# A macaron block on one core: where the bulk loads stand, three additions for four, and attention's head in the written-out order

## The reference

```
x = x + 0.5 * ffn(layernorm(x))
x = x + attn(layernorm(x))
x = x + 0.5 * ffn(layernorm(x))

ffn:  top 2 of 8 experts per row (softmax over the two logits), each expert 512 -> 256 -> gelu -> 512,
      plus a shared expert 512 -> 512 -> gelu -> 512
attn: z = causal conv, width 4, of x @ W_mem: k (32 heads x 8) and one score per head
      p = exp(clip(score) + decay);  phi = k * theta, 8 frequencies per value
      cs = cumsum(p, p*cos(phi), p*sin(phi)) over the 512 rows of a batch's sequence
      out_re = sum over m of (re*q_re + im*q_im) / den,  out_im = sum over m of (im*q_re - re*q_im) / den
      y = out_re @ W_re + out_im @ W_im per head;  y = value * silu(gate);  return y @ W_out
```

## Time and profile before

| | |
|---|---|
| median of 3 runs | 1228.48 us |
| lowest to highest | 1225.8 to 1231.84 us |
| the profiled execution, its own time | 1230.61 us |
| its span | 1229.1 us |
| TensorE busy | 1027.5 us, 84% |
| VectorE busy | 727.2 us, 59% |
| ScalarE busy | 658.5 us, 54% |
| GpSimd busy | 485.3 us, 39% |
| TensorE's granted clock, mean | 0.939 of full speed |

### The profile page before, as it was taken

The page is one execution under the profiler, slowest core; times in us unless marked ns, Lnnn a source line. Parts: engine busy times, 40 slices in busy tenths (PEclk is TensorE's granted clock), DMA queues, the critical chain, the costliest instruction groups (busy, mean ns, idle before and its releaser), DMA issues. The chain is left out here.

```text
span 1229.1 us, 11345 instructions
## 1 busy us (share of the span) xinstructions
PE 1027.5 (84%) x3424; PEld 563.1 (46%) x3424; DVE 727.2 (59%) x1206; ACT 658.5 (54%) x1112; POOL 485.3 (39%) x452
## 2 busy tenths in 40 slices
PE   4939999858999679799878979987978898679993
PEld 2526545534445445344534534444555543336661
DVE  3500016699799699689969977897979920300000
ACT  2414325578556487454866774446579851314441
POOL 4335431353533443250733312634364420165552
PEclk9969999988999889989979989899989999789997
DMA  8886571666744666843765827256686663125666
GB/s 274 320 283 113 98 163 50 170 150 119 159 126 117 181 154 109 210 115 101 202 155 106 208 77 171 53 169 139 137 188 148 101 121 70 58 64 109 112 111 103
DMA packets 68976, 172.53 MB, mean 140 GB/s; under 512 B 12354, under 2 KB 12354, under 8 KB 66790
## 3 DMA queue, kind: packets, MB, share of 16 engines
q0 software_dynamic: 32576, 72.44, 32.6%
q1 hardware_dynamic: 36342, 99.38, 26.7%
HBM read 112.86 MB, written 68.33 MB: 147 GB/s over the span
## 5 line engine op out<-in xcount | busy, mean ns | idle before, releaser
L859 PE MATMUL yps<-w_all,hidden_sb 128*128 x424 | 210.7, 621 | 43.6 <-ACT hidden_sb L1025 43.5
L843 PE MATMUL hps<-w_all,hidden_sb 128*128 x848 | 209.3, 391 | 22.5 <-ACT hidden_sb L1025 18.4
L1612 POOL DMA_INDIRECT xs<-x_normal,rows_i x106 | 131.7, 1242 | 210.4 <-PE xps L834 159.5
L843 PEld LDWEIGHTS hps<-w_all,hidden_sb 128*128 128x128 f32 x848 | 161.2, 195 | 76.5 <-issue 58.7
L1414 DVE TENSOR_TENSOR_SCAN run<-pwx,trig 128x512 f32<-128x512 f32 x128 | 149.2, 1206 | 12.8 <-ACT trig L1111 12.5
L1636 POOL DMA_INDIRECT x_rows<-ys,rows_i x56 | 100.1, 1788 | 119.3 <-ACT ys L1038 110.3
L859 PEld LDWEIGHTS yps<-w_all,hidden_sb 128*128 128x128 f32 x424 | 79.5, 197 | 120.5 <-issue 117.9
L1038 ACT ACTIVATE ys<-yps,slots 128x512 f32<-128x512 f32 x106 | 72.8, 689 | 96.2 <-PE yps L859 86.6
L801 PE MATMUL yps<-sw_sb,hidden_sb 128*128 128x512 f32 x256 | 123.9, 628 | 0.0
L789 PE MATMUL hps<-xnT,sw_sb 128*128 128x512 f32 x256 | 118.2, 610 | 0.7 <-ACT hidden_sb L998 0.7
L834 PE MATMUL xps<-ident,xs 128*128 128x128 f32 x424 | 66.5, 281 | 41.1 <-DMA xs<-x_normal,rows_i 33.5
(11 more groups left out here) (200 smaller groups left out, 1597.3 us busy)
## 6 DMA issues: line engine op xcount, KB each, us to landing
qx<-q_cols SPq DMA_DIRECT2D x128, 256.0 KB
x_normal<-xin SPq DMA_DIRECT2D x32, 256.0 KB, 4.1
w_all<-in_w_experts SPq DMA_DIRECT2D x8, 1024.0 KB, 7.3
xin<-x_rows SPq DMA_DIRECT2D x32, 256.0 KB, 7.1
turns_sb<-in_w_out SPq DMA_DIRECT2D x3, 1536.0 KB, 12.7
xin<-in_x SPq DMA_DIRECT2D x16, 256.0 KB, 4.6
sum_rows<-ys SPq DMA_DIRECT2D x16, 256.0 KB, 4.1
xin<-sum_rows POOLq DMA_DIRECT2D x16, 256.0 KB, 9.0
```

Source lines behind the costliest of these rows:

```text
L843: t = PE.matmul(hps[:, bank, 0:H], xT[:, j % 2, c, :], w_all[:, bass.ds(expert[j] + c * H, H)], start=c == 0, stop=c == KC - 1)
L859: t = PE.matmul(yps[:, bank, :], hb[:, j % 2, ec, :], w_all[:, bass.ds(expert[j] + (KC * H + ec * D), D)], start=ec == 0, stop=ec == EC - 1)
L1612: GE.indirect_dma_start(xs[:, j % NX, :], None, xn_rows[PAIR_OF[g]], bass.IndirectOffsetOnAxis(rows_i[:, g % 2, j:j + 1], 0)).then_inc(*xs ...
```

## The change

Three things. First, the start: `tables` is split. What the gate and the placement need is made first (last signal `consts` 5), the rest in `more_tables` (`consts` 6 for the zero rows, 15 the last). The expert loads go out from the first weights on, one ahead of the normalised rows' store; the block-diagonal weights and the copies of batches 1 to 3 wait for the third block's first product. Group 0's copy stands behind the experts. The scatters are planned in fours, group 1's behind `bring(0, 2)`. Second, the sums: `add_parts` does the imaginary part first and writes the real part into the other half of `qx`, so that `sum_parts` adds both with one 1,024-wide addition; the wait of a step's phases is on the additions, two steps before, for the sum. Third, all pieces of attention's head get 2,000 more in `way`.

```diff
@@ plan_weights, plan_job, plan_blocks
-            piece("POOL", ("w_rest",), 9.0, ("POOL", ("load", 0)))
+            piece("POOL", ("w_tables",), 3.0, ("POOL", ("load", 0)))
+            piece("POOL", ("w_rest",), 6.0, ("POOL", ("w_tables",)))
-                piece("SP", ("w_expert", e), 0.6, *([("SP", ("w_expert", e - 1), 4.0)] if e else [("SP", ("w_rest",))]))
-            piece("SP", ("w_bd",), 0.5, ("SP", ("w_expert", E - 1)))
+                piece("SP", ("w_expert", e), 0.6, ("SP", ("w_expert", e - 1) if e else ("w_first",), 4.4))
+            piece("SP", ("w_bd",), 0.5, ("PE", ("one", 0, 2)))
-                piece("SP", ("w_rows", b), 0.5, ("SP", ("w_expert", E - 1) if b else ("w_bias",)))
+                piece("SP", ("w_rows", b), 0.5, ("PE", ("one", 0, 2)) if b >= len(GROUPS[0]) else ("SP", ("w_expert", E - 1)))
-            piece("POOL", ("scatter", g), 2.5 * GTS[g], ("DVE", ("place", g)), *[("DVE", ("gates", q)) for q in GROUPS[g]],
-                  ("SP", ("w_rest",), 3.0))
+            for i in range(GTS[g] // 2):
+                piece("POOL", ("scatter", g, i), 5.1, ("DVE", ("place", g)), *([("POOL", ("bring", 0, 2))] if g == 1 else []),
+                      *[("DVE", ("gates", q)) for q in GROUPS[g]], ("SP", ("w_rest",), 3.0))
@@ plan_step
-            piece("DVE", ("c_sum", b, n), 2.8 if m else 1.4, ("DVE", ("c_times", b, n)),
+            piece("DVE", ("c_sum", b, n), 2.6 if m else 1.4, ("DVE", ("c_times", b, n)),
@@ orders
+            for k in work:
+                if k[1][0] in ("a_load", "a_stats", "a_norm", "a_turn", "a_mem", "a_p", "a_fall", "a_q", "a_spread"):
+                    way[k] += 2000.0
@@ tensor_program
                 pe.wait_ge(*small_loaded.at(2))
-                pe.wait_ge(*consts.at(16))
                 pe.wait_ge(*x_kept.at((q, TB - 1)))
@@ vector_program
-                    vec.wait_ge(*(out_summed if last[1] % M else added).at((*last, 0)))
+                    vec.wait_ge(*added.at((*last, 0)))
             def add_parts(b, n):
-                re = outT[:, half, 0, :] if m == 0 else re2[:, 0, :]
-                im = outT[:, half, 1, :] if m == 0 else im2[:, 0, :]
+                re, im = [outT[:, half, i, :] if m == 0 else im2[:, i, :] for i in range(2)]
                 if m == 0 and b > 0:
                     vec.wait_ge(*y_made.at((b - 1, half * VH + VH - 1)))
-                vec.wait_ge(*real_made.at((b, n)))
-                VE.tensor_tensor(re, re2[:, 0, :], re2[:, 1, :], ALU.add).then_inc(*added.of((b, n, 0)))
                 vec.wait_ge(*imag_made.at((b, n)))
                 VE.tensor_tensor(im, im2[:, 0, :], im2[:, 1, :], ALU.subtract).then_inc(*added.of((b, n, 1)))
+                vec.wait_ge(*real_made.at((b, n)))
+                vec.wait_ge(*added.at((b, n, 1)))
+                VE.tensor_tensor(re, re2[:, 0, :], re2[:, 1, :], ALU.add).then_inc(*added.of((b, n, 0)))
             def sum_parts(b, n):
-                re, im = outT[:, half, 0, :], outT[:, half, 1, :]
                 vec.wait_ge(*added.at((b, n, 0)))
-                VE.tensor_tensor(re, re, trig[:, n % 2, 0, :], ALU.add).then_inc(*out_summed.of((b, n, 0)))
-                vec.wait_ge(*added.at((b, n, 1)))
-                VE.tensor_tensor(im, im, qx[:, n % NQX, 0, :], ALU.add).then_inc(*out_summed.of((b, n, 1)))
+                VE.tensor_tensor(outT[:, half, :, :], outT[:, half, :, :], qx[:, n % NQX, :, :],
+                                 ALU.add).then_inc(*out_summed.of((b, n)))
@@ sync_program
                 elif stage == "w_bd":
+                    sp.wait_ge(*one_made.at((0, 2)))
                     SP.dma_start(wbd_sb[:, :, :, :], w_bd).then_inc(*bd_loaded.of(0))
                 elif stage == "w_rows":
+                    if at[0] >= len(GROUPS[0]):
+                        sp.wait_ge(*one_made.at((0, 2)))
```

More of the change, by code:

```diff
@@ L316, in plan_job @@
             rows, turned_rows = rows_free(("fetch", q))
-            start = [("SP", ("w_first",), 7.0), ("SP", ("w_bias",), 2.5), ("POOL", ("w_rest",))] if q == 0 else []
+            start = [("SP", ("w_first",), 7.0), ("SP", ("w_bias",), 2.5), ("POOL", ("w_tables",))] if q == 0 else []
             x_rows = [("POOL", ("o_rows", b, tb), 3.6) for tb in range(TB)] if f == 2 else []
@@ L362, in plan_blocks @@
             piece("PE", ("place", g), 2.2, ("DVE", ("rank", z)), bank=[("xps", ("DVE", ("place", g)))])
-            piece("DVE", ("place", g), 6.5, ("PE", ("place", g)),
-                  *([("PE", ("two", g - 2, NBS[g - 2] - 1)), ("POOL", ("scatter", g - 2), 2.0)] if g > 1 else []))
-            piece("POOL", ("scatter", g), 2.5 * GTS[g], ("DVE", ("place", g)), *[("DVE", ("gates", q)) for q in GROUPS[g]],
-                  ("SP", ("w_rest",), 3.0))
-            piece("SP", ("slots", g), 0.5, ("POOL", ("scatter", g), 3.0),
+            piece("DVE", ("place", g), 5.0 if NB < 16 else 6.5, ("PE", ("place", g)), *([("DVE", ("rows", 0))] if g == 1 else []),
+                  *([("PE", ("two", g - 2, NBS[g - 2] - 1)), ("POOL", ("scatter", g - 2, GTS[g - 2] // 2 - 1), 2.0)] if g > 1 else []))
+            for i in range(GTS[g] // 2):
+                piece("POOL", ("scatter", g, i), 5.1, ("DVE", ("place", g)), *([("POOL", ("bring", 0, 2))] if g == 1 else []),
+                      *[("DVE", ("gates", q)) for q in GROUPS[g]], ("SP", ("w_rest",), 3.0))
+            piece("SP", ("slots", g), 0.5, ("POOL", ("scatter", g, GTS[g] // 2 - 1), 3.0),
                   *([("ACT", ("two", g - 2, NBS[g - 2] - 1)), ("DVE", ("rows", g - 2))] if g > 1 else []))
@@ L769, in gate_logits @@
                 bank = bank_of(xps_turn, ("logits", q))
+                pe.wait_ge(*consts.at(5))
                 pe.wait_ge(*chunks_kept.at(q))
@@ L1451, in scale_output @@
                 vec.wait_ge(*spread_den.at((b, half)))
-                vec.wait_ge(*out_summed.at((b, half * M + M - 1, 1)))
+                vec.wait_ge(*out_summed.at((b, half * M + M - 1)))
                 if half:
@@ L1670, in tables @@
                 GE.tensor_tensor(chunk_sum[:, :], chunk_pairs[:, 0, :], chunk_pairs[:, 1, :], ALU.add)
+                GE.memset(earlier[:, :], 1.0).then_inc(*consts.of(2))
+                GE.memset(before[:, :, :], 1.0).then_inc(*consts.of(3))
                 GE.memset(half_pi[:, :], math.pi / 2)
@@ L1677, in tables @@
                 GE.memset(gcols[:, :, 2 * (E + 1):BR], 0.0)
-                GE.memset(no_rows[:, :, 1], 0.0)
-                GE.memset(earlier[:, :], 1.0).then_inc(*consts.of(2))
-                GE.memset(before[:, :, :], 1.0).then_inc(*consts.of(3))
-                GE.memset(rep_sb[:, :], 1.0).then_inc(*consts.of(4))
                 GE.iota(steps_of[:, :], pattern=[[P, E]], base=0, channel_multiplier=0,
@@ L1692, in tables @@
                             allow_small_or_imprecise_dtypes=True)
+                pool.wait_ge(*consts.at(3))
+                GE.affine_select(out=earlier[:, :], in_=earlier[:, :], compare_op=ALU.is_gt, fill=0.0, base=0,
+                                 pattern=[[1, P]], channel_multiplier=-1).then_inc(*consts.of(4))
+                GE.affine_select(out=before[:, :, :], in_=before[:, :, :], compare_op=ALU.is_gt, fill=0.0, base=0,
+                                 pattern=[[1, E], [-1, E]], channel_multiplier=0).then_inc(*consts.of(5))
@@ L1695, in tables @@
                 GE.iota(posn, pattern=[[1, T]], base=0, channel_multiplier=0,
-                        allow_small_or_imprecise_dtypes=True).then_inc(*consts.of(6))
-                pool.wait_ge(*consts.at(6))
-                GE.affine_select(out=earlier[:, :], in_=earlier[:, :], compare_op=ALU.is_gt, fill=0.0, base=0,
-                                 pattern=[[1, P]], channel_multiplier=-1).then_inc(*consts.of(7))
-                GE.affine_select(out=before[:, :, :], in_=before[:, :, :], compare_op=ALU.is_gt, fill=0.0, base=0,
-                                 pattern=[[1, E], [-1, E]], channel_multiplier=0).then_inc(*consts.of(8))
+                        allow_small_or_imprecise_dtypes=True).then_inc(*consts.of(9))
@@ L1735, in pool_program @@
                     own = a_norming.at((at[0], 7))
+                elif stage == "w_tables":
+                    pool.wait_ge(*own)
+                    tables()
+                    own = consts.at(5)
                 elif stage == "w_rest":
                     pool.wait_ge(*own)
-                    tables()
-                    own = consts.at(16)
+                    more_tables()
+                    own = consts.at(15)
                 elif stage == "scatter":
```

73 lines of the change are left out of this document (36 added, 37 removed).

## The result

| | before | changed |
|---|---|---|
| median | 1229.57 us | 1259.72 us |
| lowest to highest | 1225.8 to 1231.84 us | 1257.75 to 1265.54 us |
| ratio | | 1.0256, 95% interval 1.0213 to 1.0299 |
| span of the profiled execution | 1229.1 us | 1257.9 us |

The change makes the kernel 2.6% slower. I had forecast 1222 us with 1241 as the upper end, so the result lies far outside.

The account below looks back on a forecast made before the run. TensorE was taken to bound the first batch's blocks, VectorE to be nearest a bound in the running sums (107 us idle). -10 + 11 - 5 - 3 = -7 on 1230.6 us, less 2.1 for the median: 1222 us, range 1203 to 1241.

Parts of the forecast that it names:

- The start (-10): Start of the kernel: first block 22.3 us sooner, less 12 us for moved loads; net -10 us, bounds -22 and -3.
- The 10.4 us for the bulk loads: Batch 0's blocks: gathers beside the moved 6.3 MB land after 14.4 us against 4.0; the 10.4 us taken once.
- my 12 us: Batch 0's blocks: cost of the start's move, 10.4 us for bulk loads and 1.6 for scatters between adds.
- The sums (+11): VectorE's running sums: dependent additions at 0.11 us a wait make 17 us, a third falls into idle; bounds +5 and +17.
- The rival in which the waits are free: VectorE's running sums: waits on its own signals cost nothing, VectorE -3 for +11, giving 1208 us; chance 0.1.
- Heads first (-5): Attention's head earlier on all engines: -17 for row waits, +12 for the last head; together -5 us, bounds -20 and +12.
- I take half of the two, -17: VectorE in the running sums: half of its 18.9 us wait for input rows and 15.5 for summed rows is saved.
- The exposed last head, +12: Batch 3's head, after step 47 and its scaling: VectorE idles 15 us for 3.68, +12 us.
- The tail (-3): From last scaling to last group's first block: 118 us and some 2 of gaps for 122.7; -3 us, bounds -5 and +8.
- The slow rival: VectorE's queue gets longer everywhere: +16 us gives 1244.5, or 1238 if a third of the removed waits is real; chance 0.23.
- the idle time above 107 us: Running sums: VectorE's idle time staying above 107 us would decide for the slow rival.
- the 120 that I had named as a sign of being wrong: Running sums: the forecast is wrong if VectorE's idle time there is under 80 or over 120 us.

Follow-up runs that it names:

- e5: Kernel before with only the new start, old additions, no heads first, later order written out as before: 1218.35 us beside 1229.18, ratio 0.9914.
- e8: Kernel before with only the new start, old additions, no heads first, in the order the planner finds: 1213.5 us, ratio 0.9882.
- e12: The start alone in planner's order, with the bulk loads waiting for the twelfth block's first product instead of the third's: ratio 0.9866.
- e11: Kernel before, its four 512-wide additions resequenced so each sum stands right behind the part it adds; all other order same: ratio 1.0026.
- e2: Kernel before with the three additions for the four and nothing else, in its own order: 1240.5 us, ratio 1.0055.
- e6: Kernel before with the new start and the three additions, no heads first, later order written out as before: 1225.34 us, ratio 0.9957.
- e7: Kernel before with 2,000 more in `way` for all pieces of attention's head and nothing else: ratio 1.0286.
- e10: Kernel before, order written out: its own until the second batch's sums are through, then that of heads first: 1253.4 us, ratio 1.0173.
- e3: Kernel before with one number changed, the planned cost of a step's sums, 2.6 for 2.8: 1244.71 us beside 1233.44, ratio 1.0086.
- e4: Changed kernel without the 2,000 in `way` for attention's head, so new start and three additions in a free order: 1252.5 us, ratio 1.0158.
- S: The start part of the change; alone on the kernel before, ratio 0.9914 in the order of before, 0.9882 in the planner's order.
- A: The three-additions part of the change; alone on the kernel before, in the order of before, ratio 1.0055.
- H: The heads-first part of the change, 2,000 more in `way` for attention's head; alone on the kernel before, ratio 1.0286.
- e1: Changed kernel with the four old 512-wide additions back, planned costs and order of the change kept: 1257.0 us, ratio 1.0190.
- e14: Kernel before with heads first only for the pieces that a head's first steps need: 1252.1 us, ratio 1.0155.
- e9: Kernel before, order written out: that of heads first until the second batch's sums are through, then its own: 1251.9 us, ratio 1.0169.
- e15: Kernel before with heads first only for the later part of the heads: 1247.6 us, ratio 1.0139.

## Why the prediction was wrong

**The start (-10): right, in part by luck.** e5 gives -0.9%, 10.8 us. The gate's product came at 17.09 us for 17.7, the first gather at 55.72 for 53, the first block at 59.27 for 59.3. That last agreement is luck: I had TensorE's own work end at 59.3 and the gather land before it, and the reverse happened, with TensorE free at 57.3 and 1.95 us of waiting. The 10.4 us for the bulk loads were one gap of 8.5 to 10.3 us (changed kernel, e8, e12). Up to the first scan the move costs more than my 12 us: 7.0 of the 22.3 us are left there, 8.0 in e5, and e5 wins the rest later. I had read 10.4 us from the gathers' landing; e12 refutes what I expected afterwards, that another place would be cheaper.

**The sums (+11): the price right, the share too high.** A dependent wait costs 0.11 to 0.12 us (e11). The addition behind the subtraction starts 0.79 us after it, 0.19 more than the free pitch, so the step is 0.38 longer and not 0.27, and VectorE up to 21 us longer over 56 steps, where the term had 17 with the first steps. Of these about a third reaches the end, not two thirds: 7 us in e2, 7.0 between e5 and e6. The two errors partly cancel. What falls away are waits: e2's VectorE is idle 100 us for 107. The rival in which the waits are free is refuted. The Trainium skill, "VectorE: DVE Perf Modes", sections "The DRAIN you can't avoid" and "Rules for kernel authors", holds, the first section from a chain of copies, that a semaphore between chained operations adds nothing and that the count of operations is what to cut. Here three operations in a chain are slower than four interleaved ones, by 3.92 against 3.54 us. In e11 and before the same four operations run, and their order, with the two waits that it brings, makes 2.65 of 2.41.

**Heads first (-5): the wrong sign, and the step that failed.** e7 measures +34.5 us. "I take half of the two, -17" assumed that VectorE's waits for rows hang on when a head's query columns leave the row buffer. In e7 these waits are 37.5 us, in before 34.4: nothing of them goes. The exposed last head, +12 in the sum, was right in kind and too large: in the changed kernel it waits 6.49 us for 3.68, which is +3, in e7 12.7 and in e10 14.4. What I put at nothing, without a reason, is the rest of the queue. A head's pieces push blocks back on TensorE and ScalarE, and ScalarE's waves come later than VectorE's scans ask for them: 43.1 us for 12.5. The head itself gains nothing, since its rows are there only when the group of blocks before it is added; in e7 the third batch's first add is at 392 us for 380.

**A second term that was missing: the planner.** I treated the edit of the planned cost, 2.8 to 2.6, as part of the additions. e3 shows that it alone reorders the whole stage and costs 11 us, more than the additions it describes. e4 and e6, equal in their instructions, stand 2.0% apart. So the parts don't add up: S, A and H alone are -1%, +0.5% and +2.9%, which happens to be near the 2.6% measured, but taking H out of the change gives back only 1.0%, because the order that is then found is a poor one too.

**A third: TensorE's clock.** The prediction has no term for it. In the changed kernel the same 3,424 matmuls take 26.3 us more, in e7 12.6 more (1040.1 us) and in e10 22.2 more (1049.7 us). Behind the gap of 8.46 us at 95.68, for one, the granted clock is 0.50 from 91 to 100 us, the lower of its two levels, and the four second products take 3.78 us, where four like them took 1.88 at 83.39 with the clock at 1.00. In the stage of running sums the mean granted clock is 0.94 before, 0.95 in e8, 0.91 in the changed kernel, e1, e7, e10 and e14. How much of the loss this makes is not shown, since no run holds the clock, and an order can lose without it: e9 is 1.7% slower with TensorE busy 1033.0 us, e3 0.9% slower with 1031.3, while e5 is 0.9% faster with 1035.5.

**The tail (-3): nothing.** 249.8 us for 249.1, with the last group's first block at 125.2 us after the last scaling for 122.7 before.

**The slow rival** had the direction right and the idle time above 107 us as its sign; at 134 us it is past the 120 that I had named as a sign of being wrong. Its parts were not: its +16 us is half of the 30 measured, the additions land with 7 us and not 17, and batch 3's head with 3 and not 12. Its chance of 0.23 was too low. The range counted on mishaps of the size of a single wait; a reordering of a stage in which two engines are each 85% busy has a spread of its own, here from about nothing (e8 beside e5) to +2.9%.

**What stays open.** Of the orders of this stage tried here, with VectorE idle between 94 and 139 us, I can say where each waits, not why one more than another. The 34 us of e7 fall into two halves in time (e9, e10) and two in kind (e14, e15), and neither split isolates one cause.

The fastest version found is the start alone, without the new additions and without heads first: 1213.5 us beside 1229.2, 1.2% less than before and 3.6% less than the change by the ratios.

## What to carry to other kernels

Where a list scheduler sets the order, every change of a cost or a priority is a change of the whole order, and must be timed with the order held fixed and again with it free: here the free order was worth up to 2%, more than any edit of instructions. Priority for a chain helps only if the chain's first piece can start sooner; when that waits for other work, the priority holds that work up. On VectorE, interleave independent instructions before merging them: merging four additions into three in a chain made the step longer.

## What the runs showed of the hardware

A 512-wide float32 addition that needs the one ahead starts 0.72 us after it (e11), one that doesn't 0.60 to 0.61 (before, e11). A chained addition reading another pair (`qx<-trig` behind `qx<-qx`) starts after 0.79 (changed kernel); why these 0.07 more was not tried. And 6.3 MB of bulk loads, behind which an add landed after 14.8 us for 4.9, cost TensorE a gap of 8.5 to 10.3 us among the gathered blocks, whether they went out at the third block or at the twelfth. Behind such a gap TensorE's granted clock was 0.50 and four matmuls took 3.78 us for 1.88; a changed order of the same matmuls made TensorE's busy time 1053.8 us for 1027.5.
